# GpSimd waits for the landing of a row's first four scatters before it sends the other four

## The chip, the cores and the metric

The kernel runs on one core of a Trainium2 chip. The metric is the device time of one execution in microseconds (us), as the median of several runs. The profile is of one execution of its own. A change of about 0.2% is what a measurement of this kernel can tell from none.

## The reference

`x` has 8 rows (batches) of 512 tokens with 128 features. Four blocks follow one another, each with a residual:

```
x = x + attention_a(layernorm(x))            # 16 heads, causal softmax
x = x + ffn(layernorm(x))
x = x + attention_b(layernorm(x))            # linear attention, then a gated MLP
x = x + ffn(layernorm(x))

def ffn(x):                                  # x is already normalised once
    xn = layernorm(x) * gamma + beta
    scores, idx = top_k(softmax(xn @ Wr + br), 2)     # 8 experts, 2 for each token
    full_e = relu(xn @ W1_e + b1_e) @ W2_e + b2_e
    return x + sum_k scores_k * (full_idx_k - c_idx_k + c_total)

# the MLP in attention_b, on h = rmsnorm(z):
z = z + (silu(h @ Wgate) * (h @ Wup)) @ Wdown
```

## The kernel before

The kernel has four large stages one behind the other: softmax attention with the routing and experts of the first ffn, linear attention, the MLP stage with the routing and experts of the second ffn, and the combination. The change is in the MLP stage. That stage works through the 8 rows b = 0 to 7, each of NT = 4 tiles of 128 tokens. Every engine has its own program, written out by hand; the order of an engine's work is the order of its program, and semaphores tie the engines together. `LAST` is 7.

In loop b TensorE computes the gate and up products of row b in four parts (L2044, L2047), then the down projection (L2055), with small jobs of the routing in between: the rank of row b - 2 (L624 to L628), the turning of row b - 1 (L426) and its logits (L547). ScalarE takes silu of each gate part (`silu`, L2110), and waits for `gate_done` of TensorE. VectorE's program for loop b is:

```
if b >= 1: x_add(b-1)            # L2140, waits for row_done of TensorE (down projection)
           route_stats(b-1)      # L318, L323, then the base of the power (L359, L360)
gated(b, 0); gated(b, 1)         # L2168
if b >= 2: route_place(b-2)      # L636 to L661: the slots of row b-2, waits for the rank
if b >= 1: route_normalise(b-1)  # L404, waits for GpSimd's power
gated(b, 2); gated(b, 3)
if b >= 1: route_select(b-1)     # logits, softmax, top two (L557 to L616)
```

So x of a row is complete at its `x_add`, its slots are known one loop later, and its tokens are scattered after that.

GpSimd has two jobs in loop b (b = 1 to 7): `pool_power` (L365), an instruction that computes the reciprocal roots of row b - 1, and from b = 2 on `pool_scatter` of row b - 2. A scatter (`pool_scatter_one`, L675) is one indirect DMA that writes 128 rows of 130 floats, 66.6 KB, of the tile `f_xn` to `expert_in` in DRAM, at the places of one column of `f_slot`. A row has NT * TOP = 8 of them, four tiles by two experts. Each adds 16 to the semaphore `scattered[u]` when it has landed, where u = b % 3 is the row's slot in a ring of three; `landed(b, u)` is the value before row b's scatters begin. Ahead of a row's first scatter `pool_may_scatter` waits for the slots, the normalised tiles and the tags of the row, and signals once. VectorE waits for `scattered[u]` only before it writes the same ring slot again, three rows later.

The last two rows are written out: two scatters of row 6, the power of row 7, the other six of row 6, and all eight of row 7. Behind them SP waits for all scatters and loads the experts' blocks (L955); the expert stage stores its tiles with scatters of its own (L1047), before whose next use VectorE waits (L1032).

Of the kernel before, what the change touches and what calls it, by code (L numbers as in the profile page):

```python
# [17 lines left out]
NT = T // P  # L18
# [16 lines left out]
TOP = 2  # L35
# [8 lines left out]
def build_hybrid(nc, x, W_K, W_Q, W_V, W_O, attn_norm_w, Wq, Wk, Wv, Wo, out_norm_w, mlp_norm_w,  # L44
                 Wgate, Wup, Wdown, gamma, beta, Wr, br, W1, b1, W2, b2, out):
    root = ExitStack()
    with root:
# [407 lines left out]
        def begin(eng, *semaphores):  # L455
            for s in semaphores:
                eng.sem_inc(s, START)  # L457
# [12 lines left out]
        def prime(pool, *semaphores):  # L470
            for s in semaphores:
                col = primed[0]
                primed[0] += 1
                pool.dma_start(spare[:, col:col + 1], z_sb[0:1, B * NT, col:col + 1]).then_inc(s, PRIMED)
            for s in semaphores:
                pool.wait_ge(s, PRIMED)
# [581 lines left out]
        with stage(clear=False) as st:  # L1058
# [23 lines left out]
            route = Route("f1", st, bankQ)  # L1082
# [557 lines left out]
        def pool_x_plus_z(b):  # L1640
            tiles = bass.ds(b * NT, NT)
            return nc.gpsimd.tensor_tensor(x_sb[:, tiles, :], x_sb[:, tiles, :], z_sb[:, tiles, :], ALU.add)

        def pool_z_rstd(pool, b, z_mean, count):
            tiles = bass.ds(b * NT, NT)
            nc.gpsimd.tensor_scalar(mean_square[:, tiles], square_sum[:, tiles], 1.0 / D, EPS, ALU.mult,
                                    ALU.add).then_inc(z_mean, 1)
            pool.wait_ge(z_mean, count)
            return nc.gpsimd.tensor_tensor(mlp_rstd[:, tiles], mean_square[:, tiles], half[:, :], ALU.pow)
# [353 lines left out]
        def mlp_stage():  # L2003
            with stage(clear=False) as st:
# [9 lines left out]
                route = Route("f2", st, bank[7], ring=3, lean=True)  # L2014
# [11 lines left out]
                def slot_of(b):  # L2026
                    return b % route.ring

                with nc.Block(no_gpsimd_drain=True) as block:
# [164 lines left out]
                    @block.gpsimd  # L2194
                    def _(pool):
                        begin(pool, *route.of_pool)
                        prime(pool, *route.scattered)
                        pool_x_plus_z(LAST).then_inc(last_sum, 1)
                        pool.wait_ge(z_squares, 1)
                        pool_z_rstd(pool, LAST, z_mean, 1).then_inc(last_rstd, 1)  # L2200
                        for b in range(1, B):
                            route.norm.pool_power(pool, b - 1, slot_of(b - 1))
                            if b >= 2:
                                route.pool_scatter(pool, b - 2, slot_of(b - 2))
                        route.pool_scatter(pool, LAST - 1, slot_of(LAST - 1), 0, 2)
                        route.norm.pool_power(pool, LAST, slot_of(LAST))
                        route.pool_scatter(pool, LAST - 1, slot_of(LAST - 1), 2)
                        route.pool_scatter(pool, LAST, slot_of(LAST))
                        experts.pool_work(pool, experts.load_counts(pool))
# [34 lines left out]
```

## Time and profile before

| what | value |
|---|---|
| median of 3 runs | 1377.77 us (1376.88 to 1378.12) |
| the profiled execution, its own time | 1380.59 us |
| its span, first to last instruction | 1378.7 us |
| mean granted TensorE clock over the span | 0.956 |
| busy: TensorE, VectorE, ScalarE, GpSimd | 1222.3, 919.2, 823.1, 517.5 us |
| GpSimd: scatters of L675, whole kernel | 128, 127.4 us busy, mean 995 ns |
| routing loop of the MLP stage | about 1042 to 1205 us of the span |

A timeline row gives an instruction's start and duration, its engine and line, what it writes and reads, and in brackets how long its engine was idle before it and whose end released it. A GpSimd DMA's duration is what GpSimd spends on it, not its landing. The releaser is inferred from semaphore events. Where instructions of one line follow one another without a gap, one row stands for several (x4, x32).

### The profile page before, as it was taken

What the parts mean: (1) busy time and instruction counts of PE and PEld (TensorE: products, weight loads), DVE (VectorE), ACT (ScalarE), POOL (GpSimd) and SP (SyncE); (2) the same over time, 40 slices, a digit from 0 to 9 for tenths busy, and PEclk for the clock granted to TensorE, in tenths of its full rate; (3) what the DMA queues carried; (4) which work ended last, traced back from release to release, by engine and by line L of the source; (5) the groups of instructions that cost most, each with busy time, mean ns of one, the idle gap of its engine ahead of it and who ended that gap; (6) DMA issues with size and microseconds to landing.
All of it is one profiled execution on the core that took longest, in us unless ns stands there. A gap on an engine that the chain in (4) does not pass through costs nothing. (4 is left out here: it accounts for less than half of the span.)

```text
span 1378.7 us, 27110 instructions
## 1 busy us (share of the span) xinstructions
PE 1222.3 (89%) x7787; PEld 925.2 (67%) x7787; DVE 919.2 (67%) x3602; ACT 823.1 (60%) x2478; POOL 517.5 (38%) x683
## 2 busy tenths in 40 slices
PE   6999999999999998699976999999997877199990
PEld 5666666666666665499964777777774654089990
DVE  6778888888888776444436888888773655244445
ACT  5888888888888885144422565656554654044440
POOL 2112232332424242455542344443332455535550
PEclk9999999999999999799998999999998999589995
DMA  9100000000000000222221000000000000222225
GB/s 287 45 1 1 9 9 9 9 9 9 12 8 13 6 15 7 69 70 71 69 83 31 16 17 16 16 1 1 1 1 0 26 32 32 71 57 71 71 72 190
DMA packets 54445, 52.92 MB, mean 38 GB/s; under 512 B 7341, under 2 KB 43098, under 8 KB 54330
## 3 DMA queue, kind: packets, MB, share of 16 engines
q1 hardware_dynamic: 36320, 29.39, 7.6%
q0 software_dynamic: 8928, 17.84, 3.9%
q10 hardware_dynamic: 9082, 4.33, 1.1%
q8 instruction: 52, 0.85, 0.3%
q14 instruction: 63, 0.52, 0.1%
HBM read 29.48 MB, written 22.05 MB: 37 GB/s over the span
## 5 line engine op out<-in xcount | busy, mean ns | idle before, releaser
L1350 ACT ACTIVATE prob<-prob,negmax 128x512 f32<-128x512 f32 (+3 forms) x512 | 283.0, 556 | 78.7 <-DVE negmax L1449 76.8
L1449 DVE CUSTOM_DVE_ANT_0 prob<-bank,mask 128x512 f32<-128x512 f32 (+3 forms) x512 | 227.7, 482 | 51.3 <-PE bank L1159 50.9
L1526 POOL TENSOR_TENSOR Vs<-Vh_sb,rinv 128x256 f32<-128x256 f32 x128 | 78.4, 612 | 363.9 <-DVE rinv L1426 363.7
L1047 POOL DMA_INDIRECT expert_out<-f_x_yb,f_x_to x142 | 136.3, 960 | 155.9 <-DVE f_x_yb L1035 79.4
L1176 PE MATMUL bank<-prob,Vs 128*64 128x512 f32 (+3 forms) x1024 | 151.9, 439 | 0.9 <-DVE zT_lo L1421 0.9
L675 POOL DMA_INDIRECT expert_in<-f_xn,f_slot x128 | 127.4, 995 | 47.3 <-issue 29.2
L979 PE MATMUL bank<-f_x_xbT,W_sb 128*128 128x256 f32 x568 | 138.6, 388 | 1.6 <-DVE f_x_xbT L1015 1.5
L1000 ACT ACTIVATE f_x_hid<-bank,cols 128x256 f32<-128x256 f32 x144 | 63.5, 475 | 92.9 <-PE bank L979 92.9
L979 PEld LDWEIGHTS bank<-f_x_xbT,W_sb 128*128 128x128 f32 x568 | 104.6, 194 | 14.7 <-DVE f_x_xbT L1015 2.9
L1000 ACT ACTIVATE prob<-bank,cols 128x256 f32<-128x256 f32 x140 | 60.9, 475 | 83.6 <-PE bank L979 83.6
L1176 PEld LDWEIGHTS bank<-prob,Vs 128*64 128x64 f32 x1024 | 63.4, 136 | 69.4 <-issue 59.4
L1032 DVE CAST f_x_to<-f_x_this_to 128x1 int32<-128x1 f32 x142 | 21.4, 151 | 117.6 <-DMA expert_out<-f_x_yb,f_x_to 115.4
L1350 ACT ACTIVATION_READ_ACCUMULATOR prob<-prob,negmax 128x1 f32 x512 | 97.2, 190 | 0.0
L1159 PE MATMUL bank<-Q_hi,K_hi 64*128 64x512 f32 (+3 forms) x512 | 93.3, 357 | 2.7 <-DVE K_lo L1416 2.1
L1809 ACT ACTIVATE yT_hi<-bank 128x512 fp32r<-128x512 f32 x64 | 38.3, 598 | 91.3 <-PE bank L1736 91.3
L1943 DVE SCALAR_TENSOR_TENSOR z_sb<-bank,ro,z_sb 128x128 f32<-128x128 f32 x256 | 88.4, 345 | 6.3 <-POOL ro L1877 2.8
L1159 PE MATMUL bank<-Q_hi,K_lo 64*128 64x512 f32 (+3 forms) x512 | 83.6, 319 | 0.0
L1159 PE MATMUL bank<-Q_lo,K_hi 64*128 64x512 f32 (+3 forms) x512 | 83.4, 318 | 0.0
L1816 ACT ACTIVATE junk<-bank 128x128 f32<-128x128 f32 x256 | 68.7, 274 | 16.7 <-PE bank L453 4.8
L1159 PEld LDWEIGHTS bank<-Q_hi,K_hi 64*128 64x128 f32 x512 | 48.4, 183 | 44.3 <-issue 34.3
L451 PE MATMUL bank<-WVO_hi,yT_hi 128*128 128x256 f32 x256 | 74.4, 291 | 2.4 <-DVE z_sb L1943 2.4
L453 PE MATMUL bank<-WVO_hi,yT_lo 128*128 128x256 f32 x256 | 72.1, 282 | 0.0
(263 smaller groups left out, 3185.0 us busy)
## 6 DMA issues: line engine op xcount, KB each, us to landing
f_x_xb<-expert_in SPq DMA_DIRECT2D x73, 130.0 KB
b_crows<-expert_out SPq DMA_DIRECT2D x16, 256.0 KB, 2.8
c_crows<-expert_out SPq DMA_DIRECT2D x16, 256.0 KB, 4.2
expert_out<-f_x_yb,f_x_to POOLq DMA_INDIRECT x142
expert_in<-fill ACTq DMA_DIRECT2D x16, 130.0 KB, 2.3
x_sb<-in_L_attn_a_x_dram SPq DMA_DIRECT2D x8, 256.0 KB, 5.9
W_sb<-in_L_ffn_W_dram SPq DMA_DIRECT2D x1, 2048.0 KB, 10.4
expert_in<-f_xn,f_slot POOLq DMA_INDIRECT x128
```

The source lines that it names most:

```text
L451: nc.tensor.matmul(ps, lhsT_hi, rhs_hi, start=True, stop=False)
L453: return nc.tensor.matmul(ps, lhsT_lo, rhs_hi, start=False, stop=stop)
L675: pool.indirect_dma_start(xg, bass.IndirectOffsetOnAxis(ap=self.slot[:, u, t, k:k + 1], axis=0), self.norm.xn_sb[:, u, t, :], None).then_i ...
L979: nc.tensor.matmul(self.bankH[c][:, 0:BLK], W1_sb[:, e, c * P:(c + 1) * P], self.xbT[:, :], start=True, stop=True).then_inc(self.up_done[c ...
L1000: nc.scalar.activation(self.hid[:, c, :], self.bankH[c][:, 0:BLK], ACT.Relu, bias=b1_col[:, e * FC + c:e * FC + c + 1]).then_inc(self.hid_ ...
L1047: pool.indirect_dma_start(yg, bass.IndirectOffsetOnAxis(ap=self.to[:, t:t + 1], axis=0), self.yb[:, t, :], None).then_inc(self.stored[t], 16)
L1159: mm = nc.tensor.matmul(bankS[which][a][:, 0:width[i]], left[r, g % 2, tile], right[r, g % 2, 0:width[i]], start=(right is Q_hi and left i ...
L1176: mm = nc.tensor.matmul(bankZ[heads, 0:width[tiles_of(m)[which]]], Vs[:, m % 4, AT[which], heads], prob[:, m % 4, a, columns_of(m, which)] ...
L1350: nc.scalar.activation(mine, mine, ACT.Exp, scale=-1.0, bias=negmax[:, n % 4, t, a:a + 1], accum_out=rowsum[:, n % 4, t, a:a + 1]).then_in ...
L1449: nc.vector.tensor_tensor_reduce(out=prob[:, n % 4, a, columns_of(n, which)], in0=bankS[which][a][:, 0:width[i]], in1=mask[:, T - width[i] ...
L1526: nc.gpsimd.tensor_tensor(Vs[:, m % 4, :, :].rearrange("p t (a d) -> p t a d", a=2), V_sb[:, quarter % 2, small:big + 1:big - small, pair] ...
L1943: nc.vector.scalar_tensor_tensor(out=tile, in0=bankO[s % 2 * 2 + m // 2][:, o:o + D], scalar=ro[:, s % 2, m:m + 1], in1=tile, op0=ALU.mult ...
```

## The change

GpSimd's part of the MLP stage gets a local helper, used for rows 0 to 5 in place of the plain scatter of a row. It issues scatters 0 to 3, waits until `scattered[u]` has risen by 16 x 4 = 64 over its value before the row, and issues scatters 4 to 7. Only these four are in flight at the wait, so the count means that all four have landed. Rows 6 and 7 stay as they were.

```
                     @block.gpsimd
                     def _(pool):
                         begin(pool, *route.of_pool)
+
+                        def scatter_in_halves(b, u):
+                            half_of = NT * TOP // 2
+                            route.pool_scatter(pool, b, u, 0, half_of)
+                            pool.wait_ge(route.scattered[u], route.landed(b, u) + 16 * half_of)
+                            route.pool_scatter(pool, b, u, half_of)
+
                         prime(pool, *route.scattered)
...
                         for b in range(1, B):
                             route.norm.pool_power(pool, b - 1, slot_of(b - 1))
                             if b >= 2:
-                                route.pool_scatter(pool, b - 2, slot_of(b - 2))
+                                scatter_in_halves(b - 2, slot_of(b - 2))
                         route.pool_scatter(pool, LAST - 1, slot_of(LAST - 1), 0, 2)
```

## Rows read from the trace of the kernel before

**Rows 1.** The list of waits, 1030 to 1215 us: total us, times, longest.

```profile
ACT silu L2110 <- remote: 23.2, 5, 4.7
...
DVE x_sb L2140 <- remote: 13.5, 5, 2.8
```

**Rows 2.** GpSimd's timeline: start us, duration us, engine, line, operation, [idle before <- releaser].

```profile
1062.76 1.64 POOL L365 TENSOR_TENSOR f_power<-f_power,half 128x8 f32<-128x8 f32 x1 [4.97 <-DVE f_power L360]
...
1075.84 1.64 POOL L365 TENSOR_TENSOR f_power<-f_power,half 128x8 f32<-128x8 f32 x1 [11.45 <-DVE f_power L360]
...
1161.16 1.67 POOL L365 TENSOR_TENSOR f_power<-f_power,half 128x8 f32<-128x8 f32 x1 [4.18 <-DVE f_power L360]
```

**Rows 3.** The timeline of all engines, loop b = 4.

```profile
1107.50 0.69 DVE L2140 TENSOR_TENSOR x_sb<-x_sb,bank 128x512 f32<-128x512 f32 x1 [2.81 <-remote]
...
1110.09 1.67 POOL L365 TENSOR_TENSOR f_power<-f_power,half 128x8 f32<-128x8 f32 x1 [4.27 <-DVE f_power L360]
...
1111.91 0.17 DVE L661 CAST f_slot<-f_slotf 128x8 int32<-128x8 f32 x1
...
1111.99 1.11 DVE L404 TENSOR_SCALAR f_xn<-x_sb,f_mv,f_power 128x128 f32<-128x128 f32 x4
...
1112.93 1.08 POOL L675 DMA_INDIRECT expert_in<-f_xn,f_slot  x1 [1.18 <-DVE f_xn L404]
...
1114.32 0.96 POOL L675 DMA_INDIRECT expert_in<-f_xn,f_slot  x1 [0.30 <-issue]
...
1116.39 3.84 PE L2055 MATMUL bank<-Wdown_sb,act_h 128*128 128x128 f32 x32
...
1121.91 0.96 POOL L675 DMA_INDIRECT expert_in<-f_xn,f_slot  x1 [0.30 <-issue]
...
1124.57 0.69 DVE L2140 TENSOR_TENSOR x_sb<-x_sb,bank 128x512 f32<-128x512 f32 x1 [2.80 <-remote]
```

**Rows 4.** The same timeline in loop b = 1, ahead of the first scatter.

```profile
1068.90 3.84 PE L2055 MATMUL bank<-Wdown_sb,act_h 128*128 128x128 f32 x32
...
1073.27 0.68 DVE L2140 TENSOR_TENSOR x_sb<-x_sb,bank 128x512 f32<-128x512 f32 x1
```

**Rows 5.** The timeline at the end of the first stage's run of eight scatters.

```profile
556.14 0.96 POOL L675 DMA_INDIRECT expert_in<-f_xn,f_slot  x1 [0.30 <-issue]
...
558.67 0.60 ACT L780 ACTIVATE A_hi<-bank 128x512 fp32r<-128x512 f32 x1 [5.00 <-remote]
```

**Rows 6.** The timeline from row 5's last scatter to row 7's place.

```profile
1172.99 0.96 POOL L675 DMA_INDIRECT expert_in<-f_xn,f_slot  x1 [0.30 <-issue]
...
1175.60 0.19 DVE L636 TENSOR_TENSOR f_place<-bank,region_at 128x32 f32<-128x32 f32 x1 [2.87 <-remote]
...
1176.49 0.69 DVE L2140 TENSOR_TENSOR x_sb<-x_sb,bank 128x512 f32<-128x512 f32 x1
...
1179.67 1.67 POOL L365 TENSOR_TENSOR f_power<-f_power,half 128x8 f32<-128x8 f32 x1
...
1181.46 1.14 DVE L404 TENSOR_SCALAR f_xn<-x_sb,f_mv,f_power 128x128 f32<-128x128 f32 x4 [2.46 <-POOL f_power L365]
...
1181.54 1.03 POOL L675 DMA_INDIRECT expert_in<-f_xn,f_slot  x1 [0.20 <-issue]
...
1187.94 0.96 POOL L675 DMA_INDIRECT expert_in<-f_xn,f_slot  x1 [0.31 <-issue]
...
1190.08 0.19 DVE L636 TENSOR_TENSOR f_place<-bank,region_at 128x32 f32<-128x32 f32 x1 [0.17 <-PE bank L628]
```

**Rows 7.** The timeline of a scatter and who waits for it, and of the last scatter.

```profile
1262.68 0.96 POOL L1047 DMA_INDIRECT expert_out<-f_x_yb,f_x_to  x1 [1.10 <-issue]
...
1265.19 0.15 DVE L1032 CAST f_x_to<-f_x_this_to 128x1 int32<-128x1 f32 x1 [1.71 <-DMA expert_out<-f_x_yb,f_x_to]
...
1200.77 0.96 POOL L675 DMA_INDIRECT expert_in<-f_xn,f_slot  x1 [0.30 <-issue]
...
1204.64 0.39 SPq L955 DMA_DIRECT2D f_x_xb<-expert_in  x1
```

## The prediction

> **What bounds the kernel now.** The change touches one stretch, the routing loop of the MLP stage, so I read the profile for that stretch alone. The chain that ended last follows only the closing store and says nothing here. The list of waits of the stretch is the first useful view [rows 1]. ScalarE's `silu` waited 23.2 us in five places and VectorE's `x_add` (L2140) 13.5 us in five places, both for a releaser called "remote": no instruction's end in the trace fits it. In the code both wait for TensorE's signals (`gate_done`, `row_done`), and TensorE had done the work long before. Five is the number of rows b = 2 to 6, and those are the rows of the loop in which GpSimd sent eight scatters before the next `x_add`.
>
> GpSimd's timeline gives the period of the loop, from one power instruction (L365) to the next [rows 2]: 13.08 us without scatters (1062.76 to 1075.84), and (1161.16 - 1075.84) / 5 = 17.06 us with them. GpSimd itself is not full: its power at 1110.09 came after 4.27 us of idleness [rows 3]. So something between costs 4 us a row, and it is not GpSimd's queue.
>
> One row in all engines shows it [rows 3]. The down projection (L2055) starts at 1116.39 and `x_add` at 1124.57, 8.18 us later. In the row without scatters the same distance is 1073.27 - 1068.90 = 4.37 us [rows 4]. TensorE's rows last 3.84 us in both. The row's last scatter starts at 1121.91, and `x_add` 2.66 us after it. A lone scatter's landing, seen from the VectorE instruction that waits for it, is 1265.19 - 1262.68 = 2.51 us after its start [rows 7]. The same is seen at two other runs of eight: the last scatter at 556.14, ScalarE released by "remote" at 558.67, 2.53 us later [rows 5], and 1172.99 to 1175.60, 2.61 us [rows 6]. My reading is that in a long unbroken run of scatters TensorE's signals are held, and let go when the last one lands. The loop is then: power, scatters, landing, `x_add`, power.
>
> **When does the hold set in?** This decides the case. TensorE's signals do come through early in a run: L2055 at 1116.39 could start only because the work that precedes it had been signalled, 3.46 us after the first scatter at 1112.93, with three of eight sent. The signal of L2055 comes due 4.37 us later, at 1120.76, when seven have been sent and the eighth is about to be (1121.91). In the last stretch GpSimd sends two scatters, the power, then six (1181.54 to 1187.94); the place instruction (L636) then starts at 1190.08, only 2.14 us after the last of them, released by TensorE with 0.17 us of waiting [rows 6]. A run of six after a pause of 1.9 us held nothing. The scatters of the expert stages go out two at a time with gaps, as the one at 1262.68 [rows 7], and "remote" ends no wait there that I found. So four in a row, landed, and four again should stay below the onset.
>
> **The change part by part.** It adds six waits of GpSimd, one for each of rows 0 to 5 (loop b = 2 to 7); rows 6 and 7 are as before. No scatter is added or removed; the helper and the loop are laid out before the run. Nothing is moved past another queue. Queued behind each wait are the row's last four scatters, then the next row's power (its results are waited for by VectorE's L404), and in loop 7 the first two scatters of row 6.
>
> The wait itself: the fourth scatter starts 1.39 + 2 x 1.265 = 3.92 us after the first (1112.93 and 1114.32, then (1121.91 - 1114.32) / 6 each [rows 3]). The fifth came 1.27 us after it; now it comes after the landing, 2.51 us [rows 7], plus GpSimd's restart. The restart isn't shown for a bare wait. Its bounds are 0.20 us (power end 1179.67 + 1.67 to scatter 1181.54, nothing to wait for [rows 6]) and 0.85 us (slots ready 1111.91 + 0.17 to scatter 1112.93, three waits and a signal between [rows 3]); I take 0.5, between them. So 3.0 us in place of 1.27: every later scatter is 1.7 us late. If landing inside a run takes longer, the far bound is the last scatter of all, 1200.77 to the load that SP issues behind it at 1204.64, 3.87 us [rows 7]. The nearest row is the 2.51, since it too has a neighbour in flight.
>
> The Trainium skill, page "DMA: Bandwidth & Descriptors", section "Anatomy of one DMA — SWDGE (gpsimd) path", puts such a DMA at about 2.0 us fixed plus its bytes over 436 GB/s, as an estimate 2.15 us for these 66.6 KB; by that the sum below would gain 0.2 us a row. The trace's 2.51 us is a little above it and is used.
>
> The PE and DVE side without the hold: `x_add` to L404 1111.99 - 1107.50 = 4.49, L404 to L2055 4.40, L2055 to the next `x_add` 4.37 [rows 3, 4]: 13.26 us. The power must be done before L404; it may start s late. It starts 2.59 us after `x_add`, lasts 1.67, and L404 follows a late one by 0.12 us (power 1179.67 + 1.67, VectorE's L404 at 1181.46 [rows 6]). So the period is 13.15 + s where s is over 0.11.
>
> The GpSimd side: power to first scatter 2.84 - s (the scatter waits for the slots, not the power), then 3.92 + 3.0 + 3.92 + 0.96, and 0.03 to the next power: 14.67 - s. Both sides agree at s = 0.76 and a period of 13.9 us. The floor of the GpSimd side, power 1.67 + 0.20 + 11.83 = 13.7, is below it. With the restart at 0.2 it is 13.8, at 0.85 it is 14.1. GpSimd's queue thus becomes the bound, by a little: the 4.27 us of idleness that would hide the wait in the old loop goes with the stall.
>
> Five periods give 5 x (17.06 - 13.9) = 15.8 us. The last one, power 1161.16 to power 1179.67, was 18.51 us [rows 2, 6]. Now row 5's scatters end 2.08 + 11.80 = 13.88 after the power, two of row 6 end at 13.88 + 0.30 + 1.26 + 0.96 = 16.40, and the power follows at 16.43. VectorE is ready for it: place no longer idles 2.87 us, so 1175.60 - 2.87 + 0.89 + 2.59 is 15.0 after the power, 15.8 with the lag of 0.76. Gain 2.1 us. From that power on, the 25 us to SP's load are a fixed chain. Sum: 15.8 + 2.1 = 17.9 us off a span of 1378.7, so 1360.8. The profiled execution took 1380.59 with what lies around its span; the median of the runs is 1377.77, 2.8 below it. I take the gain off the median: 1359.9.
>
> **The rivals.**
> - *The hold stays (slower).* Signals may be held whenever scatters are in flight after the first few of a row, landed or not. TensorE's signal comes due about 8 us after the first scatter; the second four run from 6.9 to 11.8. If the fifth scatter already holds it, `x_add` comes 2.6 us after a last scatter that is 1.7 us later than now. Place: the ends of rows 2 to 6 and the place instruction of loop 7. Price: 6 x 1.73 = 10.4 us, 1388.2. It decides from the point where a pause for landing doesn't reset what counts the run. For it: six release times tied to the last landing. Against it: the run of six.
> - *The wait is hidden and nothing else happens.* If the "remote" stall has another cause that only falls together with the last landing (for instance the next row's own signals), GpSimd's 4.27 us of idleness [rows 3] covers 1.7 us of delay, and the time is 1377.8. In the Trainium skill the same section of the DMA page says that many descriptors can be emitted before it costs anything more; by that rule a throttle can win nothing and its result is this one. Against it: the row without scatters, in which 4 us are missing.
> - *The landing in a run takes 3.87 us.* GpSimd's floor is then 13.7 + 1.36 = 15.06; gain 5 x 2.0 + 0.7 = 10.7, 1367.1.
> - *The GpSimd queue doesn't bind.* With 13.26 us a period the gain is 19.0, and up to 3 at the end: 1355.8. It needs a landing under 2 us, which no row shows.
>
> **How the numbers follow.** The forecast 0.66, with its own range 1357.5 to 1363; long landing, or a hold gone in part of the rows, 0.12; free GpSimd 0.05; hold stays 0.10; hidden 0.07. Measurement tells about 0.2%, 2.8 us. Faster is 0.66 + 0.12 + 0.05 = 0.83, same 0.07, slower 0.10. The range reaches from the free case to a little beyond the long landing, 1355.5 to 1369, and leaves out the last two and some tail, under 2 in 10.
>
> **What would show it.** Right: no wait for "remote" in the loop; power to power 13.8 to 14.1 us in five periods; fourth scatter to fifth 3.0 us; L2055 to `x_add` near 4.4 us; GpSimd's idleness before the power near zero. Wrong: a "remote" wait that again ends 2.6 us after the eighth scatter (hold stays), a period of 17.1 with GpSimd idle 2.5 us (hidden), or a gap of over 4 us between the halves. The weakest step is the onset: I have one run of six and runs of eight, and nothing that shows a landing in the middle of a run.

## The result, and the profile after

The changed kernel took 1362.47 us (median of 4 runs, 1361.33 to 1363.59) beside 1377.39 us for the kernel before on the same chip: a ratio of 0.9880 with a 95% interval of 0.9866 to 0.9894, 14.9 us faster. The forecast was 1359.9 in a range of 1355.5 to 1369. On another chip the same pair was measured again (below): 1361.82 beside 1380.63, ratio 0.9874 (0.9854 to 0.9893), 18.8 us. The profiled executions differ by 1378.7 - 1361.0 = 17.7 us of span. The kernel before moves more from chip to chip (1377.4 to 1381.2 on four chips) than the changed one (1362.5 and 1361.8 on two); what follows compares each kernel with the one before on the same chip, by ratios, and goes by periods in the traces.

The list of waits of the changed kernel for 1030 to 1200 us names "remote" nowhere. What GpSimd and VectorE wait for instead:

```profile
POOL expert_in L675 <- DMA expert_in<-f_xn,f_slot: 11.8, 6, 3.1
...
DVE f_xn L404 <- POOL f_power L365: 7.1, 4, 4.7
```

The first line is the change itself: six scatters that wait until earlier ones have landed. The 23.2 and 13.5 us of [rows 1] are gone, and VectorE now waits for GpSimd's power, 7.1 us in four places, which it did in the kernel before only at row 7. Next, GpSimd's timeline, the powers that answer to [rows 2]:

```profile
1074.63 1.68 POOL L365 TENSOR_TENSOR f_power<-f_power,half 128x8 f32<-128x8 f32 x1 [11.46 <-DVE f_power L360]
...
1088.92 1.68 POOL L365 TENSOR_TENSOR f_power<-f_power,half 128x8 f32<-128x8 f32 x1
...
1102.37 1.68 POOL L365 TENSOR_TENSOR f_power<-f_power,half 128x8 f32<-128x8 f32 x1
...
1116.16 1.67 POOL L365 TENSOR_TENSOR f_power<-f_power,half 128x8 f32<-128x8 f32 x1
...
1131.11 1.67 POOL L365 TENSOR_TENSOR f_power<-f_power,half 128x8 f32<-128x8 f32 x1
...
1144.29 1.67 POOL L365 TENSOR_TENSOR f_power<-f_power,half 128x8 f32<-128x8 f32 x1
```

(1144.29 - 1074.63) / 5 = 13.93 us a period, where it was 17.06. The last five of the six rows show no idle time before them: the power starts as the last scatter ends. GpSimd is not without slack for all that. Behind these five powers it stands idle 0.5, 0.9, 0.6, 0.2 and 1.2 us before the row's first scatter, four times until VectorE has the slots and tiles ready, so GpSimd and VectorE bound the loop together, as the two equations of the prediction have it. One loop in all engines, to be laid beside [rows 3]:

```profile
1104.93 1.03 POOL L675 DMA_INDIRECT expert_in<-f_xn,f_slot  x1 [0.89 <-DVE f_xn L404]
...
1108.55 3.84 PE L2055 MATMUL bank<-Wdown_sb,act_h 128*128 128x128 f32 x32
...
1108.80 0.96 POOL L675 DMA_INDIRECT expert_in<-f_xn,f_slot  x1 [0.30 <-issue]
...
1111.37 0.96 POOL L675 DMA_INDIRECT expert_in<-f_xn,f_slot  x1 [1.61 <-DMA expert_in<-f_xn,f_slot]
...
1112.92 0.68 DVE L2140 TENSOR_TENSOR x_sb<-x_sb,bank 128x512 f32<-128x512 f32 x1
...
1113.29 0.60 ACT L2110 ACTIVATE silu<-bank 128x512 f32<-128x512 f32 x1 [1.24 <-PE bank L2044]
...
1115.17 0.96 POOL L675 DMA_INDIRECT expert_in<-f_xn,f_slot  x1 [0.30 <-issue]
```

The fifth scatter starts 2.57 us after the fourth, released by a DMA. The down projection starts at 1108.55 and `x_add` at 1112.92: 4.37 us, as in [rows 4], and not the 8.18 of [rows 3]. It no longer waits for anything, though two scatters of the second half have gone out by then and two are to come.

### The profile page after: what moved, and what is told of

Its sections match the earlier page's. It is cut to its first block and busy times, and to the rows that moved or that the text cites. A ratio compares the mean times of both kernels' runs of the same rounds, so it can differ in the third digit from the quotient of the medians.

```text
span 1361.0 us, 27110 instructions
## 1 busy us (share of the span) xinstructions
PE 1219.8 (90%) x7787; PEld 924.5 (68%) x7787; DVE 920.1 (68%) x3602; ACT 824.2 (61%) x2478; POOL 517.2 (38%) x683
## 5 line engine op out<-in xcount | busy, mean ns | idle before, releaser
L1000 ACT ACTIVATE f_x_hid<-bank,cols 128x256 f32<-128x256 f32 x144 | 63.6, 475 | 93.0 <-PE bank L979 93.0
L979 PEld LDWEIGHTS bank<-f_x_xbT,W_sb 128*128 128x128 f32 x568 | 104.6, 194 | 14.7 <-DVE f_x_xbT L1015 2.9
L1000 ACT ACTIVATE prob<-bank,cols 128x256 f32<-128x256 f32 x140 | 61.1, 475 | 81.7 <-PE bank L979 81.7
```

The lines of the kernel that those rows point to most:

```text
L979: nc.tensor.matmul(self.bankH[c][:, 0:BLK], W1_sb[:, e, c * P:(c + 1) * P], self.xbT[:, :], start=True, stop=True).then_inc(self.up_done[c ...
L1000: nc.scalar.activation(self.hid[:, c, :], self.bankH[c][:, 0:BLK], ACT.Relu, bias=b1_col[:, e * FC + c:e * FC + c + 1]).then_inc(self.hid_ ...
```

## The experiments

All kernels change only GpSimd's program (and add a scratch tile where one is written). "Period" is the mean of the five distances from power to power in the profiled execution, as in the result above. The kernel before took 1380.7 us (19 runs) beside the first four of them, 1381.2 (7 runs) beside the next four and 1380.6 (17 runs) beside the last four.

**The wait after the sixth scatter.**

```
-    wait after scatter 4 of 8 (rows 0 to 5)
+    wait after scatter 6 of 8
```

> The wait for landing stands after the sixth scatter of rows 0 to 5 in place of the fourth. Theory A (the hold sets in at the seventh scatter of an unbroken run, and a landing resets it): the same 1.3 us gap per row as in the changed kernel, no wait for remote in the loop, power to power 13.4 to 14.1 us, the time within 2 us of the changed kernel's 1362.5. Rival B (any scatter in flight beyond the fourth or fifth holds TensorE's signals): the signal due about 8 us after the first scatter is held until the sixth has landed at 8.9 us or later, waits for remote of some 1 us come back, period 14.5 to 15.5, time 1366 to 1371. Rival C (the hold ends only with a row's last landing): period over 17, time 1378 to 1386.

Measured: 1364.8 us, ratio 0.9890 (0.9874 to 0.9907), period 14.37. No "remote" in the loop, so by the list of waits theory A holds; the period lies above its band and just under rival B's. The timeline shows why:

```profile
1128.30 0.96 POOL L675 DMA_INDIRECT expert_in<-f_xn,f_slot  x1 [0.31 <-issue]
...
1129.03 0.29 DVE L604 TENSOR_TENSOR f_is_k<-expert_id,f_topidf 128x32 f32<-128x32 f32 x2
...
1130.42 0.19 DVE L611 TENSOR_TENSOR f_sel<-f_is_k 128x32 bf16<-128x32 f32 x1 [1.11 <-DVE f_is_k L604]
...
1130.69 0.60 ACT L2110 ACTIVATE silu<-bank 128x512 f32<-128x512 f32 x1 [1.87 <-PE bank L2044]
...
1130.77 0.68 DVE L2140 TENSOR_TENSOR x_sb<-x_sb,bank 128x512 f32<-128x512 f32 x1
1130.87 0.96 POOL L675 DMA_INDIRECT expert_in<-f_xn,f_slot  x1 [1.61 <-DMA expert_in<-f_xn,f_slot]
```

VectorE's `f_sel` waits 1.11 us for VectorE's own `f_is_k`, which ended at 1129.32; in the changed kernel this step took 0.03 us. ScalarE's `silu` comes 1.69 us after its product's start (1129.00) and not 1.06. Both are let go 2.1 to 2.4 us after the sixth scatter's start, just ahead of its landing. Signals are late with six in a row, one of VectorE too; it costs little because the landing comes soon. VectorE's step is a good gauge: in the six loops with scatters it took 0.24 to 1.10 us here and 0.29 to 1.0 in the kernel before, and 0.03 to 0.04 in the changed kernel.

`x_add` now comes 5.44 us after the down projection's start (1125.33) in place of 4.37, behind VectorE's own late signal. That sets the period: 4.49 + 4.40 + 5.44 = 14.33, and the periods on either side of this row are 14.33 and 14.35. GpSimd is not the bound here. In four of the five periods its power starts 2.57 or 2.58 us after `x_add`, as in the kernel before, and only once, behind a landing of 3.61 us, later. Rival B was nearer in mechanism, A in time. My onset of seven was too late.

VectorE's delay is not tied to the run's last landing, as TensorE's is. In the kernel before `f_sel` starts at 1120.86, 0.22 us after the seventh scatter (1120.64) and ahead of the eighth (1121.91), and in all six loops of both kernels it comes 1.3 to 2.2 us after the sixth scatter's start, whether two more follow at once or not.

**The wait after the seventh.**

```
+    wait after scatter 7 of 8
```

> The wait for landing stands after the seventh scatter. Theory A: the seventh in a row sets the hold, and the seventh's landing, about 10.3 us after the first scatter, ends it; remote waits come back with 1 to 2 us each, period 15.5 to 16, time about 1370 (1368 to 1373). Rival D (only a run of the full eight holds): no remote wait, period 13.5 to 14.1, time 1360 to 1364. Rival C (the hold ends only with the row's last landing, 12.8 us after the first scatter): period 18.3, time about 1385.

Measured: 1374.6 us, ratio 0.9954 (0.9938 to 0.9971), period 15.78. "Remote" ends `x_add`'s wait in all five rows, 1.1 to 1.9 us each:

```profile
1134.25 0.95 POOL L675 DMA_INDIRECT expert_in<-f_xn,f_slot  x1 [0.30 <-issue]
...
1136.72 0.69 DVE L2140 TENSOR_TENSOR x_sb<-x_sb,bank 128x512 f32<-128x512 f32 x1 [1.16 <-remote]
1136.79 0.95 POOL L675 DMA_INDIRECT expert_in<-f_xn,f_slot  x1 [1.58 <-DMA expert_in<-f_xn,f_slot]
```

`x_add` starts 2.41 to 2.49 us after the seventh scatter's start in four rows, with the eighth not yet sent. In the fifth it comes 3.18 us after it, 0.64 after the eighth's start, and in three rows a `silu` does the same (3.17 to 3.22). So the release goes with the landing of the scatters that are out, and not with the row's last one: rival C falls, D falls, A's mechanism and period hold. The time is 1.6 us above A's band.

**A pause that is none.**

```
-    pool.wait_ge(route.scattered[u], route.landed(b, u) + 16 * half_of)
+    nc.gpsimd.memset(paused[:, b, :], 0.0)          # 4 columns of scratch
```

> In place of the wait for landing GpSimd does one small memset (4 columns of a scratch tile) between the fourth and the fifth scatter; nothing is waited for, so the fourth has not landed when the fifth goes. Theory A as I hold it (the landing, that is nothing in flight, resets the run): the hold is back, remote waits of 2.5 and 4.5 us in five rows, period 17.3 to 17.6, time 1377 to 1381. Rival E (a pause in descriptor generation is enough): no remote wait, GpSimd's queue shorter by about 1 us a row than with the wait, period 13.2 to 13.5, time 1357 to 1360.

Measured: 1380.5 us, ratio 1.000 (0.9991 to 1.001), period 17.06. The memset took 0.13 us, and lay inside the 0.30 us that GpSimd leaves between two scatters anyway, so the fifth still came 1.26 us after the fourth:

```profile
1114.47 0.95 POOL L675 DMA_INDIRECT expert_in<-f_xn,f_slot  x1 [0.30 <-issue]
1115.41 0.13 POOL L2202 MEMSET m_paused<- 128x4 f32 x1
1115.73 0.96 POOL L675 DMA_INDIRECT expert_in<-f_xn,f_slot  x1 [0.19 <-issue]
```

It is a control: another instruction between the scatters does nothing, and the kernel is the one before to 0.1%. It says nothing on pauses, so neither A nor E is decided by it.

**Waits after two, four and six.**

```
+    for n in (2, 4, 6): scatters up to n, wait for their landing
```

> Waits for landing after the second, fourth and sixth scatter of rows 0 to 5. No hold is expected by any theory. If GpSimd's queue is the bound of the loop, as the prediction says, two more gaps of 1.3 us each are paid in full: period 16.3 to 16.8, the power starting directly behind the last scatter, time 1362.5 + 6 x 2.6 = 1378 (1375 to 1381). If the loop has slack on GpSimd's side the time stays under 1370.

Measured: 1378.6 us, ratio 0.9980 (0.9967 to 0.9992), period 17.02; no "remote" in the loop. The two further waits are paid for in full and a little more:

```profile
1126.63 0.95 POOL L675 DMA_INDIRECT expert_in<-f_xn,f_slot  x1 [0.30 <-issue]
1127.61 1.67 POOL L365 TENSOR_TENSOR f_power<-f_power,half 128x8 f32<-128x8 f32 x1
1129.47 1.03 POOL L675 DMA_INDIRECT expert_in<-f_xn,f_slot  x1 [0.20 <-issue]
```

The power starts 0.02 us after the last scatter's end and the next row's scatter 0.19 us after the power: GpSimd's queue is full in three of the five loops. In the other two its power waits 1.10 and 0.86 us for VectorE, whose `x_add` has waited 1.7 and 1.6 us for TensorE: a power that comes late in one loop holds up the next. The period is 3.09 us above the changed kernel's for two gaps of 1.3 us, and lies above the expected 16.3 to 16.8. This is the clearest evidence that GpSimd's queue counts once the hold is gone, and of what a landing costs it: 1.3 us.

**A pause without a landing.**

```
-    pool.wait_ge(route.scattered[u], route.landed(b, u) + 16 * half_of)
+    nc.gpsimd.tensor_tensor(paused[:, b, :], unit[:, :], half[:, :], ALU.pow)
```

> Between the fourth and the fifth scatter of rows 0 to 5 GpSimd does a power on a scratch tile of 4 columns (about 1.0 us, as the one at L1649) and waits for no landing; the fifth starts 2.2 us after the fourth, some 0.3 us before it has landed. Theory A1 (the landing of everything in flight resets the run): signals are held again, as with the memset whose fifth came after 1.26 us; period 17.8 to 18.2, time 1381 to 1387. Theory A2 (a stretch without a new scatter is what counts): no remote wait in the loop, the gap 0.35 us shorter than with the landing wait, period 13.3 to 13.7, time 1359 to 1364.

Measured: 1360.6 us, ratio 0.9860 (0.9836 to 0.9883), period 13.78. No "remote" in the loop. GpSimd's timeline:

```profile
1107.93 0.96 POOL L675 DMA_INDIRECT expert_in<-f_xn,f_slot  x1 [0.31 <-issue]
1108.92 1.04 POOL L2202 TENSOR_TENSOR m_paused<-unit,half 128x4 f32<-128x4 f32 x1
1110.16 1.03 POOL L675 DMA_INDIRECT expert_in<-f_xn,f_slot  x1 [0.20 <-issue]
```

The fifth starts 2.23 us after the fourth, less than the landing's 2.5, and yet the gauge step takes 0.03 to 0.04 us and nothing waits for "remote". A1 falls: not everything needs to have landed. A stretch of 2.2 us without a new scatter is enough here. The period is just above A2's 13.3 to 13.7, the time inside its band.

**Slower scatters, no pause.**

```
+    nc.gpsimd.tensor_tensor(paused[:, b, n, :], ident[:, :], keep[:, :], ALU.add)   # after each of seven
```

> After each of the first seven scatters of a row GpSimd adds two 128-column tiles into scratch (about 0.3 to 0.4 us), so the scatters of rows 0 to 5 start some 1.6 us apart instead of 1.27, with no long gap. If it is the number of scatters in an unbroken run that counts, the hold is back from the seventh on and ends with the eighth's landing: remote waits, period 19 to 19.6, time 1388 to 1394. If it is the rate (something that fills faster than it drains at 1.27 us a scatter), no remote wait, and GpSimd's queue, 2.3 us longer than before the change, sets a period of 14.3 to 14.7, time 1364 to 1370.

Measured: 1370.0 us, ratio 0.9919 (0.9903 to 0.9936), period 15.14. The scatters start 1.65 us apart, eight in a row over 11.6 to 11.7 us, and no signal of the loop is seen to be held: no "remote", and VectorE's gauge step takes 0.03 to 0.04 us. The power follows the last scatter with no idle time in four of the five periods. The period is above the expected 14.3 to 14.7 and the time at the edge of its band; each addition took 0.47 us and not 0.3 to 0.4. The count in an unbroken run is thus not what matters. The rate is: eight at 1.65 us hold nothing, six at 1.27 us do. With a landing of 2.5 us the rate also sets how many scatters are in flight at once, and the runs do not tell the two apart.

**The first stage's run of eight.**

```
 # first stage, rows 6 and 7
-    route.pool_scatter(pool, B - 2, 0)
+    scatters 0 to 3 of row 6, wait for their landing, scatters 4 to 7
     route.pool_scatter(pool, B - 1, 1)
```

> The changed kernel, and the wait for landing also between the halves of row 6 in the first stage, the other unbroken run of eight ahead of TensorE work. Theory A: ScalarE's A_hi and prob and VectorE's place of row 7 are released 2 to 2.5 us earlier there, the last eight scatters of that stage start 1.5 to 2.3 us earlier, time 1.5 to 2.3 us under the changed kernel. Rival (another engine sets that stage's end): no difference.

Measured: 1368.7 us (1364.8 to 1373.0), ratio 0.9917 (0.9891 to 0.9943): by the medians some 6 us slower than the changed kernel, though the intervals of the ratios just touch, and neither theory's number. The timeline of that stage:

```profile
553.13 0.19 DVE L636 TENSOR_TENSOR f_place<-bank,region_at 128x32 f32<-128x32 f32 x1
553.22 0.95 POOL L675 DMA_INDIRECT expert_in<-f_xn,f_slot  x1 [1.72 <-DMA expert_in<-f_xn,f_slot]
...
567.10 0.96 POOL L675 DMA_INDIRECT expert_in<-f_xn,f_slot  x1 [0.31 <-issue]
...
570.38 1.08 ACT L792 ACTIVATE WVO_hi<-bank 128x512 fp32r<-128x512 f32 x2 [16.45 <-remote]
```

The place of row 7 came at 553.13 and not at 559.17, as hoped for. So row 7's slots were ready early, and its eight scatters ran directly behind row 6's last four: twelve unbroken, 553.22 to 567.10. ScalarE stood idle for 16.45 us ahead of `WVO_hi` (L792), which was held until 3.3 us after the last. The hold had moved to the longer run and to a signal of the experts' weights.

That took the gain back. The load of the experts (L955) starts at 570.65, 3.8 us ahead of the changed kernel's 574.45. But ScalarE, late behind `WVO_hi`, issues its own DMAs (L945) until 576.04, and its first relu of the stage (L1000) starts 5.67 us after TensorE's first product (575.23 to 580.90) where it is 1.26 us in the changed kernel. TensorE waits 2.44 us for it, its granted clock goes from 1.00 in 580 to 582 us back to 0.50 in 584 to 586, and the third store of the stage starts at 589.57, against 589.50. A loss of 6 us isn't in this trace: it is of the fastest of the four executions, with a span 1.9 us above the changed kernel's. Why the others took up to 8 us more stays open.

**The end of the loop.**

```
-    row 6: scatters 0 and 1; power of row 7; row 6: scatters 2 to 7
+    power of row 7; row 6: scatters 0 to 3, wait for their landing, scatters 4 to 7
```

> The changed kernel with the end rearranged: the power of row 7 directly behind row 5's scatters, then row 6's eight scatters in halves with the wait for landing. In the changed kernel that power is ready at 1158.7 us and starts at 1161.6, behind two scatters of row 6. It should start 2.5 us earlier; row 6's scatters then end 13.2 us after it where row 7's slots are ready after 12.2, so 1.0 to 1.2 us are given back at row 7's first scatter: 1.3 to 1.5 us faster than the changed kernel. Rival: the run of four, four and then eight holds a signal of the tail, no gain or a loss.

Measured: 1362.6 us, ratio 0.9858 (0.9838 to 0.9877). GpSimd's timeline:

```profile
1145.26 1.67 POOL L365 TENSOR_TENSOR f_power<-f_power,half 128x8 f32<-128x8 f32 x1
...
1159.84 1.68 POOL L365 TENSOR_TENSOR f_power<-f_power,half 128x8 f32<-128x8 f32 x1
...
1173.28 0.96 POOL L675 DMA_INDIRECT expert_in<-f_xn,f_slot  x1 [0.30 <-issue]
```

From the power of row 6 to that of row 7 it is 14.58 us where it was 17.33, and row 7's first scatter follows 13.44 us later where it was 12.24: 1.55 us gained, as worked out. In the times it does not stand out: the interval overlaps that of the changed kernel. The trace shows that something behind it took the gain back, which the rival had named:

```profile
1173.68 15.26 ACTq L945 DMA_DIRECT2D expert_in<-fill  x8
...
1193.61 1.57 ACT L1000 ACTIVATE f_x_hid<-bank,cols 128x256 f32<-128x256 f32 x4 [24.46 <-issue]
```

Row 6's last four scatters and row 7's eight are now one run of twelve (1168.11 to 1182.13). ScalarE needs 15.3 us to issue its eight DMAs (L945) there, 11.6 in the changed kernel, and its first relu starts 4.16 us after TensorE's product (1189.45), where it was 1.26. TensorE waits 0.93 us for it, and its granted clock, 0.50 at the start of the expert stage in both kernels (the 1.2 GHz level), comes back to 1.00 about 4 us later: it is 0.78 in 1198 to 1200 us, and in the changed kernel 0.77 in 1194 to 1196. From the load of the experts (L955) to the end of the span it is 177.4 us, against 174.6. The two kernels below that have the same end show the same: 15.1 us for the DMAs and 177.0 and 177.9 to the end, where the eleven traces with the old end have 11.4 to 11.8 and 173.9 to 175.1. That the run of twelve slows ScalarE's DMAs is argued from this; no run tests it alone. In all three kernels the profiled execution is the slowest of the four, so the others may lose less.

**The changed kernel again, on another chip.**

```
(no edit)
```

> The changed kernel itself once more, beside the others of this job, since the kernel before took 1377.4 us on the first chip and 1380.7 to 1381.2 on the next. If the gain is a property of the kernel, the ratio to before is 0.986 to 0.989 and the difference 15 to 19 us wherever it runs; the prediction's 17.9 us would be a ratio of 0.987.

Measured: 1361.8 us (1361.1 to 1367.7), ratio 0.9874 (0.9854 to 0.9893), period 14.00.

**One distance of 1.65 us.**

```
-    pool.wait_ge(route.scattered[u], route.landed(b, u) + 16 * half_of)
+    nc.gpsimd.tensor_tensor(paused[:, b, :], ident[:, :], keep[:, :], ALU.add)
```

> One addition of two 128-column tiles on GpSimd between the fourth and fifth scatter of rows 0 to 5, so that this one distance is 1.65 us in place of 1.27 and all others are as before. A backlog that fills at 1.27 us a scatter and drains at 1.65 would be made shorter a little and not emptied: signals still held, remote waits in most rows, time 1370 to 1381. If any visible gap resets the count, no remote wait and the shortest GpSimd queue of all, period 13.2 to 13.5, time 3 to 5 us under the changed kernel.

Measured: 1380.7 us, ratio 1.000 (0.999 to 1.0011), period 17.09. The list of waits:

```profile
ACT silu L2111 <- remote: 18.9, 4, 4.7
DVE x_sb L2141 <- remote: 18.2, 5, 3.7
```

The fifth came 1.62 us after the fourth; `x_add` waited 18.2 us for "remote" in five rows, more than before. It starts 2.3 us after the last scatter's start (1106.99 and 1109.31 in the second row). VectorE's gauge step is back to 0.03 to 0.04 us. Its signal falls due 7.5 us after the row's first scatter, as in the kernel before, where it was late; the next of TensorE's, due 4.37 us after the down projection's start or 7.8 us after the first scatter, is held in full. A visible gap alone does not help TensorE's signals. Of the two accounts the backlog fits; that there is a backlog is not shown by it.

**Pauses in the MLP stage, and its end rearranged.**

```
+    the power on scratch in place of the wait in rows 0 to 5, then power of row 7, row 6 with the same pause
```

> The power on scratch (fifth scatter 2.2 us after the fourth) in place of the landing wait in rows 0 to 5, and the end rearranged: power of row 7 directly behind row 5, then row 6 with the same pause. Both single steps showed it: about 3.5 us off the six rows (0.33 us each, and the two slow landings of 1.5 and 0.7 us are no longer waited for) and 1.5 us at the end. Under the changed kernel by 4 to 5.5 us. Rival: GpSimd's queue is no longer the bound after the first of the two, and the second brings under 1 us.

Measured: 1361.4 us, ratio 0.9856 (0.9838 to 0.9873), period 13.79. It is not measurably faster than the changed kernel. In the trace it is 2.6 us shorter from the first power of the stage to the load of the experts (122.3 us, against 124.9 in the changed kernel and 123.1 with the pauses alone) and 2.4 us longer from there to the end, as told above. Around the end of the loop:

```profile
1154.23 1.03 POOL L675 DMA_INDIRECT expert_in<-f_xn,f_slot  x1 [0.20 <-issue]
...
1156.20 0.18 PE L628 MATMUL bank<-run_bf,ones_bf 128*128 128x32 bf16 x1
...
1157.13 0.19 DVE L636 TENSOR_TENSOR f_place<-bank,region_at 128x32 f32<-128x32 f32 x1 [0.86 <-PE bank L628]
...
1160.60 1.67 POOL L365 TENSOR_TENSOR f_power<-f_power,half 128x8 f32<-128x8 f32 x1 [1.53 <-DVE f_power L360]
```

The place instruction started 0.93 us after TensorE's rank, where it is 0.21 us in the changed kernel (1155.03 to 1155.24), and the power after it had 1.53 us of idleness before it. So a signal of TensorE came some 0.7 us late in spite of the pause of 2.2 us, and VectorE became the bound of that loop. The rival holds: beyond the pauses alone the second step brought 0.8 us up to the load.

**The first stage in four groups of four.**

```
+    first stage, rows 6 and 7: a power on scratch between each group of four scatters
```

> As the one before, and the scatters of rows 6 and 7 of the first stage in four groups of four with a power on scratch between them. With the wait only in the middle of row 6, twelve scatters ran on unbroken behind it and ScalarE's WVO_hi was held 16.4 us, so nothing was gained. With all groups broken no remote wait should be left in the first stage, its last scatter start at about 568.5 in place of 569.85 and the first load of the experts 1 to 2.5 us earlier: that much under the kernel before this one. Rival: three pauses cost GpSimd 2.9 us there and no signal ended the stage, 0 to 1.5 us slower.

Measured: 1361.9 us, ratio 0.9857 (0.9839 to 0.9876), no different from the one before. `WVO_hi` was free (its two parts started at 564.55 and 565.90, in the changed kernel at 565.52 and 568.79), but another signal was held (this kernel's lines are shifted by one):

```profile
553.85 1.03 POOL L676 DMA_INDIRECT expert_in<-f_xn,f_slot  x1 [0.19 <-issue]
...
557.72 0.95 POOL L676 DMA_INDIRECT expert_in<-f_xn,f_slot  x1 [0.30 <-issue]
...
559.71 0.17 DVE L925 COPY f_x_counts<-bank 128x8 f32<-128x8 f32 x1 [4.52 <-remote]
...
559.93 1.03 POOL L676 DMA_INDIRECT expert_in<-f_xn,f_slot  x1 [0.20 <-issue]
```

VectorE's `f_x_counts` waited 4.52 us for "remote", to 1.99 us after the eighth scatter's start, behind two groups of four with a pause between them. The load of the experts began at 574.88, against 574.45 in the changed kernel. In the kernel that waits only in row 6 the same signal was held to 558.96, and in the changed kernel it was not. A pause that served in the loop did not here.

## Why the prediction was right, point by point

- **The bound.** Right. VectorE and ScalarE waited for TensorE's held signals. With the release no longer tied to the eighth scatter the period fell from 17.06 to 13.93; and where the release was moved to the seventh's landing it fell to 15.78, 1.28 less, which is one scatter.
- **The onset.** Off. I put it at the seventh scatter, from a run of six that held nothing. The wait after the sixth showed signals 0.2 to 1.1 us late. And it isn't a count: eight at 1.65 us hold nothing. The run of six that I leaned on could not show a hold: the place instruction's signal came due there when TensorE's rank (L628) ran at 1189.86, 1.92 us after the last scatter's start, and the wait after the sixth lets signals go 1.4 to 2.4 us after it. Four with a landing are below the onset in the loop all the same. That the margin from six to four was enough is luck: two groups of four with a pause of 2.2 us held a signal in the first stage.
- **The wait's price.** The restart was taken as 0.5 us and the landing as 2.51, 3.0 together. In four of the six rows the fifth scatter came 2.54 to 2.57 us after the fourth, so with a landing of 2.51 the restart is near nothing. In the other two it took 4.07 and 3.25 us. Mean 2.9: right in sum, wrong in its parts.
- **GpSimd as the new bound.** Right, in the sense of the two equations: no idle time before the last five of the six powers, 0.2 to 1.2 us of it before the first scatters, and the waits in pairs paid for in full. The lag s of the power was taken as 0.76 and was 0.65, 0.30, 0.65, 1.79 and 0 us in the five loops. The period was forecast at 13.9 and measured 13.93; five of them gave 15.7 us for 15.8.
- **The last period.** Too high. The term was 2.1 us and measured 18.51 - 17.33 = 1.18. Most of the missing 0.9 is the lag: the sum let row 5's first scatter follow the power by 2.84 - 0.76 = 2.08 us, but the power of row 6 (1144.29) came 2.59 us after its `x_add`, with no lag, and the scatter 2.85 us after it. That is 0.77. Row 5's landing of 3.25 us adds 0.12, since the sum had 3.0 for it:

```profile
1151.06 0.96 POOL L675 DMA_INDIRECT expert_in<-f_xn,f_slot  x1 [0.31 <-issue]
...
1154.31 0.96 POOL L675 DMA_INDIRECT expert_in<-f_xn,f_slot  x1 [2.29 <-DMA expert_in<-f_xn,f_slot]
...
1161.62 1.67 POOL L365 TENSOR_TENSOR f_power<-f_power,half 128x8 f32<-128x8 f32 x1
1163.40 0.86 DVE L404 TENSOR_SCALAR f_xn<-x_sb,f_mv,f_power 128x128 f32<-128x128 f32 x3 [4.73 <-POOL f_power L365]
```

  Against the usual 2.55 the gap of 3.25 us is 0.7 too long, and it pushes the scatters behind it and the power of row 7, for which VectorE waits 4.73 us.
- **The sum.** 17.9 forecast, 17.7 between the spans of the two profiled executions (of which 1.2 lies ahead of the loop, where nothing was changed, and isn't the change's: 1062.76 against 1061.54), 14.9 and 18.8 between medians on two chips. What the trace gives to the change in the loop is 15.65 + 1.18 = 16.8 us. That the spans come so near the forecast is luck, in that the 1.2 us ahead of the loop stand in for the last period. The forecast ratio of 0.987 lies in both intervals.
- **The rivals.** The hold that stays (1388.2) and the hidden wait (1377.8) are excluded by the periods. The long landing (3.87 us) came true in two rows of six, with 4.07 and 3.25 us. The free GpSimd did not occur.

What stays open is what the hold is. The runs show that in the loop it came with scatters at 1.27 us, six or more; that it delays signals of VectorE as well as of TensorE, TensorE's the most; that TensorE's mostly get through 2.0 to 2.7 us after the start of the last scatter sent, 3.3 in the first stage's run of twelve and 3.2 in three rows of the kernel with the wait after the seventh, while VectorE's get through in the middle of a run, as one of TensorE's did (`f_x_counts` at 558.96, in that same run of twelve); and that a pause of 2.2 us clears it in the loop, all but once, and not in the first stage. A backlog would do much of this, but no row shows one: the sixth scatter of a run landed as fast as the fourth (2.57 us). The share that the DMA writes and GpSimd's own work have in it wasn't separated, and scatters held to two in flight were not tried.

## What to carry to other kernels

A wait whose releaser is "remote", in a place where the code waits for a compute engine, deserves a closer look than its length suggests: compare the same step in an iteration without the DMA traffic, and look what it is a constant distance from (here 2.5 to 2.7 us after the last scatter's start). In this kernel long unbroken runs of indirect DMAs held other engines' signals back; one wait for landing in the middle bought 3.1 us a row for 1.3 us of GpSimd's time, or more where a landing is slow. Try where to put such a break, and look again afterwards, behind the change as well as in it: removing a hold let the next run start earlier and grow longer, twice here to twelve scatters, and both times the gain was lost in the stage that followed.

## What the runs showed of the hardware that was not expected

- Signals between engines, and an engine's signal to itself, arrived late while scatters went out at 1.27 us, with no instruction record that explains it (VectorE to itself: up to 1.1 us in place of 0.03; TensorE to VectorE: `x_add` 8.2 us after the down projection's start in place of 4.4).
- In the three kernels in which twelve scatters run unbroken ahead of the last expert stage, ScalarE took 15.1 to 15.3 us to issue eight DMAs, and 11.4 to 11.8 in all others.
- A scatter's landing is 2.54 to 2.57 us after its start in most rows, and 4.07 and 3.25 us in two. These two are not chance: in the kernels with the wait after the fourth, row 3's took 4.07, 4.35, 4.48 and 4.31 us, and row 5's 3.25, 3.24, 3.06 and 3.06. The DMA view of the changed kernel for 1122.2 to 1126.4 us, the stretch of the slow one:

```profile
q0 software_dynamic: 64, 0.13, 9.9%
q8 instruction: 1, 0.02, 2.0%
```

  The 16 KB packet of the instruction queue is in both slow stretches of each of these four kernels, and in none of the four normal ones of the changed kernel. The one slow landing of the kernel with the wait after the sixth, 3.61 us, has it too. But so has a landing of 2.66 us in the kernel with three waits (1168.88 to 1171.54), so the packet alone does not make one slow. That an instruction fetch delayed the landing is argued from the coincidence, not shown by an experiment. A pause doesn't meet it, since it waits for no landing.
- The Trainium skill, page "DMA: Bandwidth & Descriptors", section "Anatomy of one DMA — SWDGE (gpsimd) path", gives about 2.0 us fixed for such a DMA, mostly completion. The trace agrees in kind: 2.54 us from start to landing, of which 0.96 on GpSimd. The same section says that many descriptors can be emitted before an added cost shows. GpSimd's queue bears it out (0.96 us for the second scatter of a run as for the eighth), the other engines' signals do not.
